# A selective scan on one core: VectorE copies y out of PSUM and makes five of sixteen input products in steps of 256 columns, and softplus is rewritten with tanh

## The chip, the cores and the metric

The kernel runs on one core of one Trainium2 chip. The metric is the device time of one execution in microseconds (us); lower is better. The time before is the median of three runs, 1869.72 us (1868.13 to 1870.24).

## The reference, cut to what matters

The model has two layers, each with cross attention, a mixer and a mixture of experts, over 128 sequences of 32 tokens of width 128. The change lies in the mixer of the second layer, a selective scan ("Mamba" style) with 256 channels, 16 states per channel and a causal convolution of 4 taps. Cut to the lines that the change touches:

```python
dt = jnp.clip(jax.nn.softplus(raw * W_dt + b_dt), 1e-4, 10.0)   # one raw value per token, 256 channels
def step(h, inp):
    dt_t, B_t, C_t, u_t = inp
    dA = jnp.exp(jnp.clip(dt_t[:, :, None] * A, -20.0, 0.0))
    dB_u = jnp.clip(dt_t[:, :, None] * B_t[:, None, :] * u_t[:, :, None], -10.0, 10.0)
    h = jnp.clip(h * dA + dB_u, -100.0, 100.0)
    y = jnp.einsum('bdn,bn->bd', h, C_t)
    return (h, y)
```

The scan runs 32 steps, one after the other. Each step updates 256 x 16 states for each of 128 sequences.

## The kernel before, in words

The kernel goes through its stages one after the other: cross attention, mixer and experts of layer 0, cross attention of layer 1, then the scan stage, then a tail with the experts of layer 1. Between stages all engines meet. An engine works through its own instructions in order, and waits on semaphores that other engines raise. All of that order is written out by hand.

The scan stage (line 1605) has two parts that matter here.

**`scan_inputs`** (line 1620) makes, for each of 32 tiles, the convolved and gated input `u`, the projections `xd` (one raw step size, 16 values of B, 16 of C per token) and the step size `dt`. It is a software pipeline: in one step of the loop, TensorE transposes and convolves one tile, ScalarE applies Silu (L1705) and copies a transpose out of PSUM (L1708), VectorE copies two PSUM results (L1780, L1783), forms the raw `dt` with `scalar_tensor_tensor` (L1785) and normalizes a later tile (`tensor_scalar` of 128 columns with two per-partition operands, L1776), and ScalarE takes the absolute value of the raw `dt` (L1712). GpSimd copies `u` away (L1746) and, in the first 12 tiles, also makes four products for the tail (L1751 to L1756). Behind the loop comes softplus, as max(x, 0) + ln(1 + exp(-|x|)): ScalarE runs Exp and Ln over 2048 columns at a time (L1733, L1737), half of the tiles after the other, and VectorE adds and clips (L1802, L1804).

**`scan_states`** (line 1810) is the scan. A position is one time step. Its 16 states are four groups of four (`q` = 0 to 3), so that a group is 1024 columns. At position `t`:

- ScalarE makes for each group the four decays exp(dt * A) of position `t` (L1897, 256 columns each, into a PSUM ring of three) and, for groups 0 to 2, the four raw products dt*u*B of position `t+1` (L1907). At the end of a position it copies y of position `t-2` out of PSUM (L1913).
- VectorE makes for each group `kept` (L1951, decay times state) and, one group behind, `state` (L1960, add and clip). The raw products of group 3 are VectorE's own: one `tensor_tensor` of 1024 columns, `mine` (L1942), in group 0 of a position.
- GpSimd clips the raw products (`bound`, L1862, 1024 columns), spreads C onto diagonals (`diagonals`, L1867, 512 columns) and makes dt*u of two positions ahead (`dt_u`, L1853), all nine in a fixed order per position: bound 0, diagonal 0, bound 1, diagonal 1, dt_u, bound 2, diagonal 2, bound 3, diagonal 3. A `bound` waits for its raw products.
- TensorE adds up y with the diagonals (L1995). The first group of a position waits until the y buffer of two positions before has been copied out.

`OWN` (L1597) says how many of the four products of each group are VectorE's. `state` of a group waits for `bound`, so for GpSimd; the decays of a group wait for the `state` three groups back, because the PSUM ring has three places.

Of the kernel before, what the change touches and what calls it, by code (L numbers as in the profile page):

```python
# [1619 lines left out]
def scan_inputs(nc, g, uz, dt, xd, a):  # L1620


    with ExitStack() as ctx:
# [25 lines left out]
        waited, abs_sb, exp_sb, ln_sb, soft_sb, clip_sb = (sem(n) for n in ("waited", "abs_sb", "exp_sb", "ln_sb", "soft_sb", "clip_sb"))  # L1649
# [15 lines left out]
        def _(pe):  # L1665
# [30 lines left out]
            pe.wait_ge(prep, TAPS + 2 + 9)  # L1696
# [3 lines left out]
        def _(act):  # L1700
            def step(t, p):
                if inside(t + 1):
                    act.wait_ge(conv_psum, t + 2)
                    wait(act, uz_sb, t)
                    nc.scalar.activation(u[(p + 1) % 2][:, :], c_ps[(p + 1) % 2][:, :], ACT.Silu).then_inc(u_sb, 1)  # L1705
                if inside(t + 2):
                    act.wait_ge(xT_psum, t + 3)
                    nc.scalar.activation(xnT[(p + 2) % TAPS][:, :], x_ps[:, 0:P], ACT.Copy).then_inc(xT_sb, 1)  # L1708
                if inside(t - 2):
                    act.wait_ge(dt_sb, t - 1)  # L1710
                    act.sem_inc(waited, 1)
# [12 lines left out]
            pipeline(act, step, 2, 2, TAPS)  # L1724

            act.wait_ge(abs_sb, T)
            act.wait_ge(a_step, 1)
            nc.scalar.activation(a[:, :], a[:, :], ACT.Exp).then_inc(a_step, 1)
            for half in range(2):
                quarters = range(half * LN_Q // 2, (half + 1) * LN_Q // 2)  # L1730
                for q in quarters:
                    s = slice(q * LT, (q + 1) * LT)
                    nc.scalar.activation(soft[:, s, :], soft[:, s, :], ACT.Exp, scale=-1.0).then_inc(exp_sb, 1)  # L1733
                for q in quarters:
                    s = slice(q * LT, (q + 1) * LT)
# [72 lines left out]


def scan_states(nc, g, uz, dt, xd, a):  # L1810
# [7 lines left out]
    with ExitStack() as ctx:  # L1818
# [69 lines left out]
        def _(act):  # L1888
# [21 lines left out]
            def keep_y(t, k):  # L1910
                act.wait_ge(y_psum, t * NQ + NQ)
                act.sem_inc(waited_act, 1)
                nc.scalar.activation(dt[:, t, :], y_ps[k % 2][:, 0:DI], ACT.Copy).then_inc(y_sb, 1)  # L1913

            def position(t, k, first=False, last=False):
                for q in range(NQ):
# [791 lines left out]
```

## Time and profile before

| | us |
|---|---|
| median of three runs | 1869.72 |
| the profiled execution's own time | 1870.31 |
| span of its profile | 1868.5 |
| TensorE busy in the span | 1580.0 (85%) |
| VectorE busy | 1353.5 (72%) |
| ScalarE busy | 1034.3 (55%) |
| GpSimd busy | 521.2 (28%) |

The profile counts its time from the start of the span. In its views PE is TensorE, DVE VectorE, ACT ScalarE and POOL GpSimd; L1942 is line 1942 of the kernel. Shares over the whole span mix stages with different limits, so the stage of the change has to be read by itself: the input loop lies at about 1030 to 1150 us, softplus at 1150 to 1175 us, the scan at 1175 to 1547 us and the tail behind it.

### The profile page before, as it was taken

Reading aid. Unit: us, or ns where it says so; the run is one execution under the profiler, and the core shown is the slowest. Engines: PE = TensorE matmul, PEld = TensorE weight load, DVE = VectorE, ACT = ScalarE, POOL = GpSimd, SP = SyncE. Lnnn points to the kernel's source line nnn. Section 1 sums busy time; section 2 is a strip of 40 time slices with the busy share of each in tenths; the row PEclk is TensorE's granted clock in tenths of the full one; section 3 lists DMA queues with packets and bytes.
Section 4 is the critical chain, followed back from the end, with each engine's and each line's share of the span. In section 5 each row is a group of like instructions: output and inputs, shape, how many; then the busy total and the mean of one; then the engine's idle time right before and its main releaser. Section 6 shows DMA issues by size and latency. Waiting matters only on the chain. (4 is left out here: it accounts for less than half of the span.)

```text
span 1868.5 us, 36875 instructions
## 1 busy us (share of the span) xinstructions
PE 1580.0 (85%) x10997; PEld 1031.1 (55%) x11024; DVE 1353.5 (72%) x3801; ACT 1034.3 (55%) x2779; POOL 521.2 (28%) x559
## 2 busy tenths in 40 slices
PE   5999999999998999799895885477777774999999
PEld 2666666666665455466563674366655563444444
DVE  4777777777777666577686444799999996677765
ACT  2666666666665333344332225899999992322321
POOL 1211111111111100000000721688888880322200
PEclk9999999999999999899897898798988886999999
DMA  5011011011010900000366000000000001000000
GB/s 136 24 34 34 23 34 34 23 34 34 23 34 5 349 8 0 1 1 1 97 212 183 0 0 0 1 1 0 0 0 0 0 0 51 1 7 6 12 6 17
DMA packets 69336, 66.48 MB, mean 36 GB/s; under 512 B 5695, under 2 KB 66834, under 8 KB 69266
## 3 DMA queue, kind: packets, MB, share of 16 engines
q1 hardware_dynamic: 66598, 64.00, 11.5%
q10 hardware_dynamic: 2668, 1.62, 0.3%
q8 instruction: 35, 0.57, 0.1%
q14 instruction: 35, 0.29, 0.0%
HBM read 61.41 MB, written 4.19 MB: 35 GB/s over the span
## 5 line engine op out<-in xcount | busy, mean ns | idle before, releaser
L1995 PE MATMUL ss_y_ps<-ss_h,ss_diag 128*128 128x256 f32 x1024 | 264.4, 422 | 133.8 <-ACT sc_dt L1913 93.2
L1995 PEld LDWEIGHTS ss_y_ps<-ss_h,ss_diag 128*128 128x128 f32 x1024 | 215.6, 214 | 182.4 <-issue 79.1
L595 ACT ACTIVATE x_probs<-x_probs,x_neg_max 128x257 f32<-128x257 f32 x512 | 253.5, 498 | 63.2 <-DVE x_neg_max L696 63.2
L696 DVE CUSTOM_DVE_ANT_0 x_probs<-x_s_ps,x_mask_b 128x257 f32<-128x257 f32 x512 | 187.3, 423 | 133.5 <-PE x_s_ps L403 133.5
L1897 ACT ACTIVATE ss_decay<-sc_dt,sc_a 128x256 f32 (+1 forms) x496 | 207.8, 479 | 1.8 <-DVE ss_h L1960 1.8
L1951 DVE SCALAR_TENSOR_TENSOR ss_decay<-ss_decay,ss_h 128x1024 f32<-128x1024 f32 x124 | 152.3, 1228 | 27.7 <-ACT ss_decay L1897 27.4
L1907 ACT ACTIVATE ss_come<-ss_dtu,sc_xd 128x256 f32<-128x256 f32 x384 | 163.6, 512 | 6.6 <-POOL ss_dtu L1853 6.6
L413 PE MATMUL x_pT_ps<-all_ident,x_probs 128*128 128x128 f32 x1024 | 162.4, 282 | 0.6 <-DVE x_pT L703 0.6
L1867 POOL TENSOR_TENSOR ss_diag<-all_ident,sc_xd 128x512 f32<-128x512 f32 x128 | 158.8, 1240 | 12.8 <-PE ss_y_ps L1995 2.9
L703 DVE COPY x_pT<-x_pT_ps 128x512 f32<-128x512 f32 x256 | 161.3, 668 | 0.5 <-PE x_pT_ps L413 0.5
L1960 DVE CUSTOM_DVE_ANT_0 ss_h<-ss_come,ss_decay 128x1024 f32<-128x1024 f32 x124 | 149.9, 1209 | 0.0
L319 POOL TENSOR_TENSOR x_rsum_b<-x_rsum,x_one_col 128x512 f32<-128x512 f32 x32 | 33.3, 1041 | 408.7 <-DVE x_rsum L713 408.7
L1862 POOL TENSOR_SCALAR ss_come<-ss_come 128x1024 f32<-128x1024 f32 x124 | 131.3, 1059 | 39.9 <-ACT ss_come L1907 34.3
L413 PEld LDWEIGHTS x_pT_ps<-all_ident,x_probs 128*128 128x128 f32 x1024 | 115.1, 144 | 45.3 <-issue 43.1
L2484 DVE TENSOR_TENSOR tl_scaled<-tl_xnT,tl_w_ps 128x512 f32<-128x512 f32 x96 | 65.4, 687 | 53.0 <-PE tl_w_ps L2200 35.9
L2206 PE MATMUL tl_h_ps<-tl_scaled,tl_w 128*128 128x512 f32 x192 | 98.6, 595 | 0.4
L2206 PE MATMUL tl_y_ps<-tl_scaled,tl_w 128*128 128x512 f32 x192 | 97.5, 592 | 0.8 <-DVE tl_scaled L2484 0.4
L595 ACT ACTIVATION_READ_ACCUMULATOR x_probs<-x_probs,x_neg_max 128x1 f32 x512 | 96.3, 188 | 0.0
L403 PE MATMUL x_s_ps<-x_kT,x_qblk 32*128 32x257 f32 x1024 | 92.7, 431 | 0.0
L390 PE MATMUL x_m_ps<-x_w_qkv,x_ctx_t 128*128 128x128 f32 x512 | 75.1, 291 | 18.2 <-issue 17.2
L430 PE MATMUL x_o_ps<-x_pT,x_v 128*32 128x128 f32 x2048 | 82.5, 279 | 0.9 <-DVE x_pT L703 0.9
L374 PE MATMUL x_m_ps<-x_ctx_t,x_w_qkv 128*128 128x512 f32 x128 | 71.4, 640 | 11.8 <-DVE x_o_norm L719 11.8
(373 smaller groups left out, 3072.0 us busy)
## 6 DMA issues: line engine op xcount, KB each, us to landing
x_ctx_t<-ctxT SPq DMA_DIRECT2D x48, 514.0 KB, 3.8
kept_ctx_t<-ctxT SPq DMA_DIRECT2D x16, 514.0 KB, 8.2
kept_ctx_n<-ctx SPq DMA_DIRECT2D x16, 512.0 KB, 8.5
x_ctx_n<-ctx SPq DMA_DIRECT2D x16, 512.0 KB, 4.1
all_x<-x SPq DMA_DIRECT2D x4, 512.0 KB, 7.8
x_mid<-all_x SPq DMA_DIRECT2D x32, 64.0 KB, 4.0
all_x<-x_mid SPq DMA_DIRECT2D x4, 512.0 KB, 7.6
out<-all_x SPq DMA_DIRECT2D x8, 256.0 KB, 2.0
```

The lines of the kernel that those rows point to most:

```text
L413: ins = tr(pT_ps[u % 2][:, n * P:(n + 1) * P], probs[p][:, 2 * u + j, k * P:(k + 1) * P], g.ident[:, :])
L595: ins = nc.scalar.activation(probs[p][:, n, :], probs[p][:, n, :], ACT.Exp, scale=-1.0, bias=neg_max[p][:, n:n + 1], accum_out=sums[p][:, ...
L696: vec.tensor_tensor_reduce(probs[p][:, n, :], s_ps[:, c, 0:S2], mask_b[:, :], -1.0, -MASKED, ALU.add, ALU.min, neg_max[p][:, n:n + 1]).the ...
L703: vec.tensor_copy(pT[u % 4][:, :], pT_ps[u % 2][:, :]).then_inc(pT_sb, 1)
L1862: nc.gpsimd.tensor_scalar(c[:, :, :], c[:, :, :], 10.0, -10.0, ALU.min, ALU.max).then_inc(bound_sb, 1)
L1867: nc.gpsimd.tensor_tensor(diag[q][:, :, :], g.ident[:, :].unsqueeze(1).to_broadcast([P, NH, P]), c.unsqueeze(2).to_broadcast([P, NH, P]), ...
L1897: ins = nc.scalar.activation(decay[r][:, m * DI:(m + 1) * DI], dt[:, t, :], ACT.Exp, scale=a[:, s:s + 1])
L1907: ins = nc.scalar.activation(come[q][k % 2][:, m, :], dtu[k % 2][:, :], ACT.Copy, scale=xd[:, t, s:s + 1])
L1951: vec.scalar_tensor_tensor(d[:, :], d[:, :], TINY, h[q][:, :, :].rearrange("p m d -> p (m d)"), ALU.max, ALU.mult).then_inc(kept_psum, 1)
L1960: vec._custom_dve(bass.dve_ops.TENSOR_ADD_SAT, out=h[q][:, :, :].rearrange("p m d -> p (m d)"), in0=come[q][k % 2][:, :, :].rearrange("p m ...
L1995: ins = nc.tensor.matmul(y_ps[p][:, 0:DI], diag[q][:, m, :], h[q][:, m, :], start=(q == 0 and m == 0), stop=(q == NQ - 1 and m == NH - 1))
L2206: mm([h_ps, y_ps][j // ME][:, :], w[:, j, :], scaled[j % 4][:, :], start=(j == 0), stop=(j == ME - 1 or j == MC - 1)).then_inc(product, 1)
```

## The change

In the scan, the copy of y moves from ScalarE to VectorE and comes one position earlier (y of `t-1` at the end of position `t`). VectorE's own products become five instead of four: one of group 2 and all four of group 3. Each is now a `tensor_scalar` of 256 columns, with a per-partition operand from `xd` and a `min` with 10, where there was one `tensor_tensor` of 1024 columns. The lone step of group 2 stands in group 0 of a position, the four of group 3 in group 1. ScalarE makes three products of group 2 instead of four.

In the input loop, VectorE clips the raw `dt` (one more `tensor_scalar` of 256 columns) and ScalarE takes Tanh of half the absolute value. With s = 0.5 + 0.5 * tanh(|x|/2), softplus is max(x, 0) - ln(s). So the loop is followed by Ln alone (no Exp), and by one VectorE instruction per quarter instead of two.

```diff
-OWN = (0, 0, 0, 4)
+OWN = (0, 0, 1, 4)
+DT_LOW, DT_HIGH = float(np.log(np.expm1(1e-4))), float(np.log(np.expm1(10.0)))
...
 # scan_inputs, ScalarE, in the loop
                     nc.scalar.activation(soft[:, t - 2, :], dt[:, t - 2, :], ACT.Abs).then_inc(abs_sb, 1)
+                if inside(t - 3):
+                    act.wait_ge(abs_sb, t - 2)
+                    act.sem_inc(waited, 1)
+                    nc.scalar.activation(soft[:, t - 3, :], soft[:, t - 3, :], ACT.Tanh, scale=0.5).then_inc(tanh_sb, 1)
...
 # scan_inputs, ScalarE, behind the loop
-            act.wait_ge(abs_sb, T)
+            for q in range(LN_Q):
+                t = slice(q * LT, (q + 1) * LT)
+                act.wait_ge(tanh_sb, (q + 1) * LT)
+                nc.scalar.activation(soft[:, t, :], soft[:, t, :], ACT.Ln, scale=0.5, bias=half[:, :]).then_inc(ln_sb, 1)
             act.wait_ge(a_step, 1)
             nc.scalar.activation(a[:, :], a[:, :], ACT.Exp).then_inc(a_step, 1)
-            for half in range(2):
...
-                    nc.scalar.activation(soft[:, s, :], soft[:, s, :], ACT.Exp, scale=-1.0).then_inc(exp_sb, 1)
...
-                    nc.scalar.activation(soft[:, s, :], soft[:, s, :], ACT.Ln, bias=1.0).then_inc(ln_sb, 1)
...
 # scan_inputs, VectorE, in the loop and behind it
-                                             ALU.mult, ALU.add).then_inc(dt_sb, 1)
+                                             ALU.mult, ALU.add).then_inc(raw_sb, 1)
+                    dve.wait_ge(raw_sb, t)
+                    vec.tensor_scalar(dt[:, t - 1, :], dt[:, t - 1, :], DT_LOW, DT_HIGH, ALU.max, ALU.min).then_inc(dt_sb, 1)
...
-                vec.scalar_tensor_tensor(dt[:, s, :], dt[:, s, :], 0.0, soft[:, s, :], ALU.max, ALU.add).then_inc(soft_sb, 1)
-                dve.wait_ge(soft_sb, q + 1)
-                vec.tensor_scalar(dt[:, s, :], dt[:, s, :], 1e-4, 10.0, ALU.max, ALU.min).then_inc(clip_sb, 1)
+                vec.scalar_tensor_tensor(dt[:, s, :], dt[:, s, :], 0.0, soft[:, s, :], ALU.max, ALU.subtract).then_inc(soft_sb, 1)
...
 # scan_states, ScalarE
-                    if q == NQ - 1 and not first:
-                        keep_y(t - 2, k)
...
 # scan_states, VectorE
-                m = OWN[q]
-                weight = xd[:, t, 1 + q * NH:1 + q * NH + m]
-                vec.tensor_tensor(come[q][k % 2][:, 0:m, :], dtu[k % 2][:, :].unsqueeze(1).to_broadcast([P, m, DI]),
-                                  weight.unsqueeze(2).to_broadcast([P, m, DI]), ALU.mult).then_inc(mine_sb, 1)
+                for m in range(OWN[q]):
+                    s = 1 + q * NH + m
+                    ins = vec.tensor_scalar(come[q][k % 2][:, m, :], dtu[k % 2][:, :], xd[:, t, s:s + 1], 10.0,
+                                            ALU.mult, ALU.min)
+                ins.then_inc(mine_sb, 1)
+
+            def keep_y(t, k):
+                dve.wait_ge(y_psum, t * NQ + NQ)
+                vec.tensor_copy(dt[:, t, :], y_ps[k % 2][:, 0:DI]).then_inc(y_sb, 1)
...
                     if not last and q < len(BY_DVE):
                         mine(t + 1, k + 1, BY_DVE[q])
+                    if q == NQ - 1:
+                        keep_y(t - 1, k - 1)
```

The rest of the diff is the semaphores' names, a constant tile `half` (one more small memset) and the last y copy.

## Rows read from the trace of the kernel before

**Rows 1.** Busy time by stretch, the scan (stretch, length, engines' busy us, PE clock)
```profile
1175.00:1547.00 372.00, 264.44 (x1024) 215.61 (x1024) 332.02 (x286) 361.74 (x913) 312.12 (x284) 0.89 0.00 0
```
**Rows 2.** Timeline (start us, us, engine, line), ScalarE, one position of the scan
```profile
1381.39 0.40 ACT L1913 ACTIVATE sc_dt<-ss_y_ps 128x256 f32 x1
1381.65 1.69 ACT L1897 ACTIVATE ss_decay<-sc_dt,sc_a 128x256 f32 x4
...
1392.83 0.40 ACT L1913 ACTIVATE sc_dt<-ss_y_ps 128x256 f32 x1
```
**Rows 3.** Timeline, VectorE, in the same position (idle before, releaser in brackets)
```profile
1387.42 1.23 DVE L1951 SCALAR_TENSOR_TENSOR ss_decay<-ss_decay,ss_h 128x1024 f32<-128x1024 f32 x1
1388.56 1.21 DVE L1960 CUSTOM_DVE_ANT_0 ss_h<-ss_come,ss_decay 128x1024 f32<-128x1024 f32 x1
...
1392.96 1.23 DVE L1951 SCALAR_TENSOR_TENSOR ss_decay<-ss_decay,ss_h 128x1024 f32<-128x1024 f32 x1 [0.84 <-ACT ss_decay L1897]
```
**Rows 4.** Timeline, GpSimd, in the same position: bound 1, diagonal 1, dt_u
```profile
1388.49 1.04 POOL L1862 TENSOR_SCALAR ss_come<-ss_come 128x1024 f32<-128x1024 f32 x1
...
1389.62 1.04 POOL L1867 TENSOR_TENSOR ss_diag<-all_ident,sc_xd 128x512 f32<-128x512 f32 x1
...
1390.62 0.74 POOL L1853 TENSOR_TENSOR ss_dtu<-sc_dt,sc_uz 128x256 f32 x1
```
**Rows 5.** Timeline, VectorE's product and GpSimd's diagonal of group 0, in the same position
```profile
1386.28 1.23 DVE L1942 TENSOR_TENSOR ss_come<-ss_dtu,sc_xd 128x1024 f32<-128x1024 f32 x1 [0.15 <-DVE ss_h L1960]
1386.29 2.12 POOL L1867 TENSOR_TENSOR ss_diag<-all_ident,sc_xd 128x512 f32<-128x512 f32 x1
```
**Rows 6.** Timeline, VectorE and GpSimd in the input loop, at three places
```profile
1032.20 0.35 DVE L1776 TENSOR_SCALAR si_xn<-all_x,all_rstd,all_shift 128x128 f32<-128x128 f32 x1 [0.56 <-PE si_x_ps L1672]
...
1053.13 0.61 DVE L1785 SCALAR_TENSOR_TENSOR sc_dt<-si_w_dt,sc_xd,si_b_dt 128x256 f32 x1 [0.16 <-DVE sc_xd L1783]
1053.54 0.79 POOL L1756 TENSOR_TENSOR sc_q<-sc_q,sc_uz 128x256 f32<-128x256 f32 x1
1053.67 0.74 DVE L1776 TENSOR_SCALAR si_xn<-all_x,all_rstd,all_shift 128x128 f32 x1
...
1139.21 0.92 DVE L1785 SCALAR_TENSOR_TENSOR sc_dt<-si_w_dt,sc_xd,si_b_dt 128x256 f32<-128x256 f32 x1
1139.24 0.62 POOL L1746 COPY sc_uz<-si_u 128x512 f32 x1 [2.96 <-ACT si_u L1705]
```
**Rows 7.** Groups of VectorE by line and shape (count | busy us, mean ns | idle before)
```profile
L1780 DVE COPY si_uT<-si_u_ps 128x256 f32<-128x256 f32 x32 | 13.6, 424 | 57.1 <-PE si_u_ps L1687 57.1
...
L1571 DVE TENSOR_SCALAR x_neg<-x_neg,x_c 128x1 f32<-128x1 f32 x32 | 6.9, 214 | 1.1
...
L1804 DVE TENSOR_SCALAR sc_dt<-sc_dt 128x2048 f32<-128x2048 f32 x4 | 4.9, 1227 | 0.1
...
L1981 DVE TENSOR_SCALAR ss_h<-ss_come 128x1024 f32<-128x1024 f32 x4 | 2.7, 692 | 1.9 <-ACT ss_come L1907 1.8
```
**Rows 8.** Timeline from the last step of the input loop to the scan's first instruction
```profile
1149.15 0.42 ACT L1712 ACTIVATE si_soft<-sc_dt 128x256 f32<-128x256 f32 x1 [0.56 <-DVE sc_dt L1785]
...
1156.01 3.71 ACT L1737 ACTIVATE si_soft<-si_soft 128x2048 f32<-128x2048 f32 x2
1157.95 2.29 DVE L1802 SCALAR_TENSOR_TENSOR sc_dt<-sc_dt,si_soft 128x2048 f32<-128x2048 f32 x1 [8.91 <-ACT si_soft L1737]
...
1175.52 1.41 POOL L1853 TENSOR_TENSOR ss_dtu<-sc_dt,sc_uz 128x256 f32<-128x256 f32 x2 [28.69 <-SPq L1818]
```
**Rows 9.** Timeline, the load of a function table in front of the scan's first decays
```profile
1186.07 1.28 ACT L1897 ACT_TABLE_LOAD   x1
```
**Rows 10.** Timeline, Silu in one step of the input loop
```profile
1134.82 0.60 ACT L1705 ACTIVATE si_u<-si_c_ps 128x512 f32<-128x512 f32 x1 [2.51 <-PE si_c_ps L1681]
```
**Rows 11.** Groups of ScalarE: table loads by line (L1259 is a Silu, beside Sigmoid)
```profile
L1259 ACT ACT_TABLE_LOAD x8 | 10.3, 1283 | 0.1
...
L1705 ACT ACT_TABLE_LOAD x1 | 1.3, 1283 | 0.0
```

More of the change, by code:

```diff
@@ L1639, in scan_inputs @@
         soft = sb("soft", [P, T, DI])
+        half = sb("half", [P, 1])
         x_ps, c_ps, u_ps, d_ps = (ps(n, [P, BANK]) for n in ("x_ps", "c_ps", "u_ps", "d_ps"))
@@ L1648, in scan_inputs @@
         waited_pool = sem("waited_pool")
-        waited, abs_sb, exp_sb, ln_sb, soft_sb, clip_sb = (sem(n) for n in ("waited", "abs_sb", "exp_sb", "ln_sb", "soft_sb", "clip_sb"))
+        waited, abs_sb, tanh_sb, ln_sb, soft_sb, raw_sb = (sem(n) for n in ("waited", "abs_sb", "tanh_sb", "ln_sb", "soft_sb", "raw_sb"))
         block = ctx.enter_context(nc.Block())
@@ L1694, in step @@
                     ins.then_inc(xd_psum, 1)
-            pe.wait_ge(prep, TAPS + 2 + 9)
+            pe.wait_ge(prep, TAPS + 3 + 9)
             pipeline(pe, step, 2, 1, TAPS)
@@ L1723, in _ @@
             norm_coefficients(nc, g, act, None, ln_step, lnw)
-            pipeline(act, step, 2, 2, TAPS)
-            act.wait_ge(abs_sb, T)
+            pipeline(act, step, 2, 3, TAPS)
+            for q in range(LN_Q):
+                t = slice(q * LT, (q + 1) * LT)
+                act.wait_ge(tanh_sb, (q + 1) * LT)
+                nc.scalar.activation(soft[:, t, :], soft[:, t, :], ACT.Ln, scale=0.5, bias=half[:, :]).then_inc(ln_sb, 1)
             act.wait_ge(a_step, 1)
             nc.scalar.activation(a[:, :], a[:, :], ACT.Exp).then_inc(a_step, 1)
-            for half in range(2):
-                quarters = range(half * LN_Q // 2, (half + 1) * LN_Q // 2)
-                for q in quarters:
-                    s = slice(q * LT, (q + 1) * LT)
-                    nc.scalar.activation(soft[:, s, :], soft[:, s, :], ACT.Exp, scale=-1.0).then_inc(exp_sb, 1)
-                for q in quarters:
-                    s = slice(q * LT, (q + 1) * LT)
-                    act.wait_ge(exp_sb, q + 1)
-                    nc.scalar.activation(soft[:, s, :], soft[:, s, :], ACT.Ln, bias=1.0).then_inc(ln_sb, 1)
         @block.gpsimd
@@ L1791, in _ @@
             vec.memset(cb[:, :], 0.0).then_inc(prep, 1)
+            vec.memset(half[:, :], 0.5).then_inc(prep, 1)
             dve.wait_ge(w_in, 16 * W_LOADS)
@@ L1795, in _ @@
             vec.tensor_scalar(a[:, :], a[:, :], 5.0, None, ALU.min).then_inc(a_step, 1)
-            dve.wait_ge(prep, 2)
-            split_row(vec, dve, prep, TAPS + 2, cb3[:, :], rowmask, (c_hi[:, :], c_rest[:, :], c_f[:, :]), cb[0:3, :])
+            dve.wait_ge(prep, 3)
+            split_row(vec, dve, prep, TAPS + 3, cb3[:, :], rowmask, (c_hi[:, :], c_rest[:, :], c_f[:, :]), cb[0:3, :])
             pipeline(dve, step, 3, 1, TAPS)
@@ L1801, in _ @@
                 dve.wait_ge(ln_sb, q + 1)
-                vec.scalar_tensor_tensor(dt[:, s, :], dt[:, s, :], 0.0, soft[:, s, :], ALU.max, ALU.add).then_inc(soft_sb, 1)
-                dve.wait_ge(soft_sb, q + 1)
-                vec.tensor_scalar(dt[:, s, :], dt[:, s, :], 1e-4, 10.0, ALU.max, ALU.min).then_inc(clip_sb, 1)
+                vec.scalar_tensor_tensor(dt[:, s, :], dt[:, s, :], 0.0, soft[:, s, :], ALU.max, ALU.subtract).then_inc(soft_sb, 1)
             dve.wait_ge(a_step, 2)
             vec.tensor_scalar(a[:, :], a[:, :], -1.0, None, ALU.mult).then_inc(a_step, 1)
-            dve.wait_ge(clip_sb, LN_Q)
+            dve.wait_ge(soft_sb, LN_Q)
 def scan_states(nc, g, uz, dt, xd, a):
@@ L1908, in raw @@
                 ins.then_inc(raw_sb, 1)
[L1910 to L1913, printed above, removed]
             def position(t, k, first=False, last=False):
@@ L1926, in _ @@
             positions(act, position)
-            keep_y(T - 2, 0)
-            keep_y(T - 1, 1)
         @block.vector
@@ L1985, in _ @@
             state(T - 1, T - 1, L)
+            keep_y(T - 1, T - 1)
+            dve.wait_ge(y_sb, T)
         @block.tensor
```

## The prediction, made before the changed kernel was built

> **What bounds the kernel now.** I read the busy time by stretch first. The scan takes 372 us, and in it ScalarE is busy 361.74, VectorE 332.02 and GpSimd 312.12 us [rows 1]: three engines close together, ScalarE in front. Next I read the timeline of one position. From one y copy on ScalarE to the next are 1392.83 - 1381.39 = 11.44 us [rows 2], which is the period. The y copy itself costs 0.26 (next start minus own start), so the 28 other instructions cost (11.44 - 0.26) / 28 = 0.399 each. ScalarE has no gap; VectorE waits for it, 0.84 us at one place of the position [rows 3]. So ScalarE bounds a position, with VectorE about 1.1 us behind it.
>
> The third view is VectorE and GpSimd beside each other. Some of their instructions exclude one another. The product of 1024 columns (L1942) starts at 1386.28 and takes 1.23; the diagonal that starts 0.01 later takes 2.12 where another takes 1.04 [rows 5, 4]: it has waited for the product's end. The input loop shows the same for a `tensor_scalar` with per-partition operands, the class of instruction that the change puts into the scan: L1776 takes 0.35 alone [rows 6]. Started at 1053.67 beside a GpSimd instruction of 1053.54 to 1054.33, it takes 0.74 and ends at 1054.41, 0.08 after GpSimd's end. `kept` and `state`, which have an operand in PSUM, keep 1.23 and 1.21 beside a busy GpSimd [rows 3, 4].
>
> **The change, part by part.**
>
> *ScalarE in the scan* loses the y copy and one product: 0.26 + 0.40 = 0.66 a position. Its floor becomes 27 x 0.399 = 10.77 us.
>
> *VectorE in the scan, without waits.* An instruction starts 0.09 before the one ahead of it has ended (1387.42 + 1.23 against 1388.56 [rows 3]), so a long one costs 1.14 and eight of them 9.12. The y copy is like L1780, 0.42 [rows 7], so 0.33. A step of 256 columns: the groups of 2048 and 1024 columns give (1227 - 692) / 1024 = 0.52 ns a column and a fixed 157 ns; one column with one operand is 214, so the operand adds 57 [rows 7]. That makes 0.157 + 0.134 + 0.057 = 0.35, or 0.26 in a chain. Five cost 1.30. The sum is 9.12 + 0.33 + 1.30 = 10.75, level with ScalarE's floor. Without any waits, nothing is lost.
>
> The Trainium skill, "VectorE: DVE Perf Modes", in the section on the TRN2 errata, gives 58 + columns/2 cycles for such a copy, and advises tiles of 512 columns and more; at 0.96 GHz that is 0.19 us a step, an estimate. By it the sum would be about 0.3 us a position lower; no row here has a step of just this form.
>
> *VectorE in the scan, with waits.* GpSimd's order is unchanged: eight instructions of 1.04 and one of 0.74 a position, about 0.08 apart [rows 4], some 9.8 us of work. Each of the five steps must find it between two instructions. A step that has waited ends 0.08 + 128 x 0.52 ns = 0.15 after GpSimd's end (the 0.08 from L1776 [rows 6], for 128 columns). The next step starts 0.09 before that, so 0.06 after GpSimd's end; GpSimd's next starts 0.08 after it. Which of the two goes first? L1785, with one operand, started at 1139.21, GpSimd's copy at 1139.24, and L1785 still waited: it took 0.92 and ended 0.27 after the copy [rows 6]. The product without an operand started 0.01 ahead and went first [rows 5]. I read this as the operand's load standing before the claim. So a step with an operand that starts 0.02 ahead loses, and each of the four in the chain waits for one whole GpSimd instruction.
>
> I lay the position out that way. The chain of four falls on diagonal 1, dt_u, bound 2, diagonal 2. The first waits for the rest of a diagonal (0.77, which I take as three quarters), then come one of 0.74 and two of 1.04, each with the gap of 0.08 between GpSimd's instructions: 0.77 + 0.15 + 0.81 + 1.12 + 1.12 = 3.97. The lone step waits for the rest of a diagonal too, 0.81 in all. VectorE: 9.12 + 0.33 + 3.97 + 0.81 = 14.23 a position. It is then the bound, ScalarE waits for `state` through the ring of three, and GpSimd for ScalarE. Against 11.44 that is +2.79 in each of the 30 positions that make a next product: +83.7 us. Bounds, by the first wait of each group (none, or a whole 1.04): 13.0 to 14.8 a position, so +47 to +101.
>
> *The scan's start.* Two of its 24 first products leave ScalarE (0.8), and the table load of 1.28 in front of the first decays [rows 9] goes, because the last function in front of the scan becomes Exp. -2.1; with the load kept, -0.8.
>
> *Softplus.* From the end of the last absolute value (1149.57) to the scan's first instruction (1175.52) are 25.95 us [rows 8]. After: one more VectorE step, a handoff and Tanh at the drain (0.35 + 0.05 + 0.42, about 0.8), a table load 1.28, the first Ln 1.90 (two take 3.71), then four VectorE instructions of 2.29, which are longer than Ln and hide the other three and the Exp of `a`: 9.2; `a` times -1 and the handoff 0.6. Together 13.8, so -12.2. Bounds: if Ln and VectorE did not overlap at all, 5.6 less gain; above, -13.
>
> *The input loop.* ScalarE is idle 2.51 us in each step of 3.58 before Silu [rows 10], so a Tanh of 0.42 fits, taken as 0. VectorE's new clip is one step of 0.35 that can wait for GpSimd's copy (0.62) or product (0.73); the absolute value reads `dt` one step later, so it is covered. While GpSimd is full, in the first 12 tiles, it loses 0.15 a tile at worst: 0 to +2, I take 0.
>
> **Sum.** +83.7 - 2.1 - 12.2 = +69.4 against the profiled execution's 1870.3 us (span 1868.5 and 1.8 around it), so 1939.7. The median of the runs is 0.6 lower: 1939.
>
> **Rivals.**
>
> *The steps of a chain go through together*, VectorE keeping its turn: the race above is 0.02 us. Then a chain costs one wait: 0.92 + 3 x 0.26 = 1.70 and the lone step 0.81, so 11.96 a position, and +15.6 - 2.1 - 12.2 = +1.3: 1871.6, from 1866 to 1882 with the first waits half or full. For it: the product of [rows 5] went first with a lead of 0.01. Against it: L1785 with a lead of 0.03 did not, and L1776 at 1053.67, right behind L1785, let GpSimd in. Chance 0.2, of which 0.09 within 0.2%, 0.07 above and 0.04 below. The Trainium skill, "SBUF — State Buffer" (section "Who interferes with whom"), has a rule for it: whichever issues first gets the shared ports for the whole instruction. By that rule this rival would hold, since the step starts first; the row at 1139.21 speaks against it.
>
> *Faster: the steps find no GpSimd in their way*, because it idles for ScalarE's products when they come (0.2 to 0.65 us at a time, now), or because a `tensor_scalar` of this form doesn't exclude it. Then the floor of 10.77 decides, to about 10.95 with handoffs: 30 x -0.6 = -18, with the rest -32: 1838. It decides once the waits of both groups together stay below 0.9 us a position. Against it: GpSimd works 9.8 us of each position, and the same class waited in [rows 6]. Chance 0.15.
>
> *The change doesn't do what it says in the input loop*: Tanh may not be in Silu's table. Sigmoid and Silu in turn cost a load each time, 8 for L1259 [rows 11]. Two loads of 1.28 and the two functions in the 2.78 us that ScalarE has there would add 0.6 to 2.6 us a step, 19 to 82 us, on top of the forecast: 1958 to 2021. The one load for the loop's Silu, Copy and Abs [rows 11] says nothing of Tanh. Chance 0.05. The Trainium skill, "ScalarE: Activation LUTs" (section "Table sets: the hidden batching unit"), lists tanh beside exp and beside sigmoid and doesn't list Silu's set; no row here shows it.
>
> **How the numbers follow.** The forecast has 0.6: 1939, its own range 1903 to 1957 by the bounds. The range reaches down through the second case, to 1866, and leaves out the faster one and the loads (0.2 together): 1866 to 1957. 0.2% is 3.7 us, about what a measurement here can tell. Faster: 0.15 + 0.04 = 0.19. Same: 0.09. Slower: 0.6 + 0.07 + 0.05 = 0.72.
>
> **What the profile after would show.** Right: 160 `tensor_scalar` of 256 columns on VectorE with a mean near 0.95 us, not 0.35; dt_u on GpSimd 14.2 us apart; ScalarE idle before decays, waiting for `state`; GpSimd idle for ScalarE's products; 13 to 14 us between the loop and the scan; one table load in the loop. Wrong: steps of 0.35, with a period near 10.9 (third case), or one long step in four with a period near 12 (second). Table loads beside Tanh would be the last case.

## The result, and the profile after

The changed kernel takes 1924.1 us (median of four runs, 1921.84 to 1926.92) against 1869.98 for the kernel before (four runs): a ratio of 1.0289, with an interval of 1.027 to 1.0309. It is 54 us slower, where 69 were forecast. The profiled execution has a span of 1920.0 us against 1868.5, so +51.5.

Where these 51.5 us lie is read by cutting the span at the scan's first instruction and at the end of its last y copy. Busy time by stretch of the changed kernel (stretch, length, then busy us with the number of instructions for PE, PE loads, DVE, ACT, POOL, then PE clock): softplus, scan, tail.

```profile
1148.04:1160.80 12.76, 0.00 (x0) 0.00 (x0) 8.98 (x5) 10.46 (x7) 0.00 (x1) 0.50 0.00 0
1160.80:1599.37 438.57, 296.80 (x1024) 231.96 (x1024) 430.19 (x444) 340.94 (x848) 288.22 (x284) 0.84 0.00 0
1599.37:1920.00 320.63, 279.36 (x960) 138.38 (x960) 231.16 (x829) 85.25 (x145) 47.56 (x23) 0.95 0.04 15
```

The scan starts at 1160.80 instead of 1175.52 [rows 8]: 14.7 us earlier. It takes 438.6 us instead of 371.6 (1175.52 to 1547.07 before), so 67.0 more. The tail takes 0.8 less. In the scan of before, ScalarE was busy 361.74 of 372 us [rows 1]; now VectorE is busy 430.19 of 438.57, or 98%, and ScalarE has 98 us of idle time. The bound has moved.

The groups say what fills VectorE and what the others wait for (line, engine, operation, tiles, count | busy us, mean ns | idle before, releaser):

```profile
L1898 ACT ACTIVATE ss_decay<-sc_dt,sc_a 128x256 f32 (+1 forms) x496 | 205.7, 459 | 88.6 <-DVE ss_h L1957 88.6
L1863 POOL TENSOR_SCALAR ss_come<-ss_come 128x1024 f32<-128x1024 f32 x124 | 129.1, 1042 | 130.6 <-ACT ss_come L1908 122.1
L1934 DVE TENSOR_SCALAR ss_come<-ss_dtu,sc_xd 128x256 f32<-128x256 f32 x160 | 140.0, 923 | 1.2 <-POOL ss_dtu L1854 1.2
```

The 160 steps (L1934) have a mean of 0.923 us. ScalarE idles 88.6 us for `state` ahead of decays, GpSimd 122.1 us for ScalarE's products. The timeline shows two positions (start us, us, engine, line; idle before in brackets), VectorE and GpSimd:

```profile
1392.83 0.41 DVE L1940 COPY sc_dt<-ss_y_ps 128x256 f32 x1
...
1394.35 1.04 POOL L1863 TENSOR_SCALAR ss_come<-ss_come 128x1024 f32<-128x1024 f32 x1 [3.60 <-ACT ss_come L1908]
1395.43 0.34 DVE L1934 TENSOR_SCALAR ss_come<-ss_dtu,sc_xd 128x256 f32<-128x256 f32 x1
1395.46 1.21 POOL L1868 TENSOR_TENSOR ss_diag<-all_ident,sc_xd 128x512 f32<-128x512 f32 x1
...
1397.54 1.04 POOL L1863 TENSOR_SCALAR ss_come<-ss_come 128x1024 f32<-128x1024 f32 x1 [0.87 <-ACT ss_come L1908]
1398.02 3.69 DVE L1934 TENSOR_SCALAR ss_come<-ss_dtu,sc_xd 128x256 f32<-128x256 f32 x4
1398.66 1.04 POOL L1868 TENSOR_TENSOR ss_diag<-all_ident,sc_xd 128x512 f32<-128x512 f32 x1
1399.66 0.77 POOL L1854 TENSOR_TENSOR ss_dtu<-sc_dt,sc_uz 128x256 f32 x1
1400.52 1.04 POOL L1863 TENSOR_SCALAR ss_come<-ss_come 128x1024 f32<-128x1024 f32 x1
...
1406.14 0.41 DVE L1940 COPY sc_dt<-ss_y_ps 128x256 f32 x1
...
1408.74 1.23 DVE L1934 TENSOR_SCALAR ss_come<-ss_dtu,sc_xd 128x256 f32<-128x256 f32 x1
1408.77 1.04 POOL L1868 TENSOR_TENSOR ss_diag<-all_ident,sc_xd 128x512 f32<-128x512 f32 x1
...
1411.96 1.04 POOL L1868 TENSOR_TENSOR ss_diag<-all_ident,sc_xd 128x512 f32<-128x512 f32 x1
1412.15 3.99 DVE L1934 TENSOR_SCALAR ss_come<-ss_dtu,sc_xd 128x256 f32<-128x256 f32 x4
...
1414.94 1.04 POOL L1868 TENSOR_TENSOR ss_diag<-all_ident,sc_xd 128x512 f32<-128x512 f32 x1
...
1420.58 0.41 DVE L1940 COPY sc_dt<-ss_y_ps 128x256 f32 x1
```

The chain of four takes 3.69 or 3.99 us. At 1398.02 its steps wait for bound 1 (its rest), diagonal 1, dt_u and bound 2, at 1412.15 for diagonal 1 (its rest), dt_u, bound 2 and diagonal 2, one each. The bounds and diagonals keep their 1.04 there [rows 4]: GpSimd gets its turn after every step. The lone step goes both ways with the same lead of 0.03 us in these rows: at 1395.43 it goes first, takes 0.34, and the diagonal waits (1.21); at 1408.74 it waits for the whole diagonal (1.23). The position takes 13.31 us after a won race and 14.44 after a lost one. From the third y copy to the thirtieth the mean is 13.76; in the kernel before, the same distance is 11.43 to 11.54 as long as a position makes a next product, 11.44 in the mean.

Softplus, from the loop's last Tanh to the scan's first instruction:

```profile
1147.33 0.70 ACT L1718 ACTIVATE si_soft<-si_soft 128x256 f32<-128x256 f32 x2
1148.06 1.28 ACT L1735 ACT_TABLE_LOAD   x1
1149.35 7.68 ACT L1735 ACTIVATE si_soft<-si_soft,si_half 128x2048 f32<-128x2048 f32 x4
1151.38 8.90 DVE L1805 SCALAR_TENSOR_TENSOR sc_dt<-sc_dt,si_soft 128x2048 f32<-128x2048 f32 x4 [4.49 <-ACT si_soft L1735]
...
1157.05 1.28 ACT L1737 ACT_TABLE_LOAD   x1
...
1160.80 1.41 POOL L1854 TENSOR_TENSOR ss_dtu<-sc_dt,sc_uz 128x256 f32<-128x256 f32 x2 [16.76 <-SPq L1819]
```

VectorE's four instructions run 2.03 behind the four Ln and hide the last three of them and the Exp of `a`.

### The profile page after: what moved, and what is told of

It is laid out like the page before. It is cut to its first block and busy times, and to the rows that moved or that the text cites. A ratio compares the mean times of both kernels' runs of the same rounds, so it can differ in the third digit from the quotient of the medians.

```text
span 1920.0 us, 37197 instructions
## 1 busy us (share of the span) xinstructions
PE 1609.8 (84%) x11024; PEld 1044.9 (54%) x11024; DVE 1461.5 (76%) x3990; ACT 1013.2 (53%) x2740; POOL 497.3 (26%) x559
## 5 line engine op out<-in xcount | busy, mean ns | idle before, releaser
L1996 PE MATMUL ss_y_ps<-ss_h,ss_diag 128*128 128x256 f32 x1024 | 296.8, 455 | 156.3 <-DVE ss_h L1957 131.5
L1996 PEld LDWEIGHTS ss_y_ps<-ss_h,ss_diag 128*128 128x128 f32 x1024 | 232.0, 232 | 220.8 <-DVE ss_h L1957 139.3
L1898 ACT ACTIVATE ss_decay<-sc_dt,sc_a 128x256 f32 (+1 forms) x496 | 205.7, 459 | 88.6 <-DVE ss_h L1957 88.6
L1863 POOL TENSOR_SCALAR ss_come<-ss_come 128x1024 f32<-128x1024 f32 x124 | 129.1, 1042 | 130.6 <-ACT ss_come L1908 122.1
L1908 ACT ACTIVATE ss_come<-ss_dtu,sc_xd 128x256 f32<-128x256 f32 x352 | 149.1, 494 | 4.3 <-POOL ss_dtu L1854 4.3
L1934 DVE TENSOR_SCALAR ss_come<-ss_dtu,sc_xd 128x256 f32<-128x256 f32 x160 | 140.0, 923 | 1.2 <-POOL ss_dtu L1854 1.2
L1868 POOL TENSOR_TENSOR ss_diag<-all_ident,sc_xd 128x512 f32<-128x512 f32 x128 | 135.7, 1061 | 12.2 <-PE ss_y_ps L1996 2.3
L2201 PE MATMUL tl_w_ps<-tl_wT,tl_spread 128*128 128x512 bf16 x192 | 74.1, 387 | 14.5 <-DVE tl_scaled L2485 12.4
```

Source lines behind the costliest of these rows:

```text
L1868: nc.gpsimd.tensor_tensor(diag[q][:, :, :], g.ident[:, :].unsqueeze(1).to_broadcast([P, NH, P]), c.unsqueeze(2).to_broadcast([P, NH, P]), ...
L1898: ins = nc.scalar.activation(decay[r][:, m * DI:(m + 1) * DI], dt[:, t, :], ACT.Exp, scale=a[:, s:s + 1])
L1908: ins = nc.scalar.activation(come[q][k % 2][:, m, :], dtu[k % 2][:, :], ACT.Copy, scale=xd[:, t, s:s + 1])
L1934: ins = vec.tensor_scalar(come[q][k % 2][:, m, :], dtu[k % 2][:, :], xd[:, t, s:s + 1], 10.0, ALU.mult, ALU.min)
L1996: ins = nc.tensor.matmul(y_ps[p][:, 0:DI], diag[q][:, m, :], h[q][:, m, :], start=(q == 0 and m == 0), stop=(q == NQ - 1 and m == NH - 1))
```

## The experiments

Twelve kernels were run. The times of before, measured beside each, are 1869.5 (e1 to e4), 1869.6 (e5 to e8), 1866.6 (e9 to e11) and 1867.1 (e12).

| kernel | us | ratio to before | us a position |
|---|---|---|---|
| changed kernel | 1924.1 | 1.0289 [1.027, 1.0309] | 13.31 or 14.44 |
| e1 one product, as before | 1856.1 | 0.9934 [0.9917, 0.995] | 11.46 |
| e2 softplus alone | 1854.8 | 0.9921 [0.9905, 0.9938] | 11.44 |
| e3 steps alone | 1920.8 | 1.0278 [1.0261, 1.0296] | 13.31 |
| e4 y copy alone | 1870.2 | 1.0004 [0.9994, 1.0014] | 11.46 |
| e5 steps with an operand in PSUM | 1853.7 | 0.9916 [0.9899, 0.9932] | 11.34 |
| e6 steps with a constant | 1886.1 | 1.0087 [1.0069, 1.0105] | 12.32 |
| e7 chain alone, in group 0 | 1854.0 | 0.9914 [0.9896, 0.9932] | 11.32 |
| e8 light GpSimd | 1857.6 | 0.994 [0.9924, 0.9957] | 11.44 |
| e9 chain first, then lone step | 1859.0 | 0.9962 [0.9948, 0.9977] | 11.58 |
| e10 all five in group 0 | 1859.9 | 0.9958 [0.9941, 0.9974] | 11.58 |
| e11 chain alone, in group 1 | 1885.2 | 1.0097 [1.008, 1.0114] | 12.46 |
| e12 four steps with PSUM, in group 0 | 1851.4 | 0.9916 [0.9902, 0.9929] | 11.22 |

The last column is the distance of two y copies in most positions; four near the scan's end, behind the loop in the code, take 13.37 in e6 and 12.01 in e8. Where the times of before differ (e9 to e12), kernels are compared by their distance from the time of before that was measured beside each.

**The parts of the change (e1 to e4).** e1 is the changed kernel with

```diff
-OWN = (0, 0, 1, 4)
+OWN = (0, 0, 0, 4)
...
-                for m in range(OWN[q]):
-                    s = 1 + q * NH + m
-                    ins = vec.tensor_scalar(come[q][k % 2][:, m, :], dtu[k % 2][:, :], xd[:, t, s:s + 1], 10.0,
-                                            ALU.mult, ALU.min)
-                ins.then_inc(mine_sb, 1)
+                m = OWN[q]
+                weight = xd[:, t, 1 + q * NH:1 + q * NH + m]
+                vec.tensor_tensor(come[q][k % 2][:, 0:m, :], dtu[k % 2][:, :].unsqueeze(1).to_broadcast([P, m, DI]),
+                                  weight.unsqueeze(2).to_broadcast([P, m, DI]), ALU.mult).then_inc(mine_sb, 1)
```

> The changed kernel with VectorE's products put back to one tensor_tensor of 1024 columns (group 3 alone); the y copy on VectorE and softplus by tanh stay. Theory (each step of 256 columns waits for its own GpSimd instruction): one product waits once at most. ScalarE has 28 instructions a position, 28 x 0.399 = 11.17 us, VectorE 9.12 + 0.33 + 1.14 = 10.6, so ScalarE bounds: 11.2 to 11.5 a position against 11.44 before, with softplus and the table load 14 to 16 us less: 1846 us, from 1844 to 1862. Rival (the y copy on VectorE is what stretches the position, since it waits for TensorE): the period stays above 13, and the time above 1900.

e2 takes `scan_inputs` from the changed kernel and the scan from the kernel before.

> The kernel before with the new input loop and softplus alone. Theory: the stretch from the loop's end to the scan is 13 us instead of 26, the scan's first decays find the table of Exp loaded (1.28 us), the scan's period stays at 11.44: 1854 us, from 1852 to 1858, with the first dt_u near 1160.8. Rival (the clip and Tanh lengthen the input loop): above 1860.

e3 is the kernel before with the changed kernel's `OWN` and the other half of e1's diff, reversed.

> The kernel before with the five steps of 256 columns alone; y copy and softplus as before. Theory: VectorE bounds at the changed kernel's 13.9 us a position less the y copy's 0.33, so 13.5: 30 x 2.1 = 63 us more, 1932 us, from 1920 to 1940. Rival (the y copy is the cost): at most 1885.

e4 is the kernel before with `keep_y` taken from ScalarE's block and put into VectorE's, as in the change.

> The kernel before with the y copy on VectorE alone. Theory: ScalarE loses 0.26 a position and still bounds at 11.2: 30 x 0.26 = 8 us less, 1862 us, from 1860 to 1870. Rival (the y copy waits for TensorE on VectorE and stretches the position): above 1880.

The steps are the cost: alone they add 51.3 us (e3), and without them the changed kernel falls by 68 (e1). Softplus alone gives 14.7 back (e2), as much as the scan's earlier start in the profile. The y copy alone gives nothing (e4), where 8 us were expected. The reason stands in the groups of e4, VectorE's product of 1024 columns and the copy:

```profile
L1933 DVE TENSOR_TENSOR ss_come<-ss_dtu,sc_xd 128x1024 f32<-128x1024 f32 x32 | 57.0, 1783 | 5.7 <-DVE ss_h L1955 4.0 <-POOL ss_dtu L1853 1.2
...
L1938 DVE COPY sc_dt<-ss_y_ps 128x256 f32 x24 | 10.0, 418 | 0.0
```

and in the timeline of e1, whose scan has the same position of 11.46 us:

```profile
1372.13 1.04 POOL L1868 TENSOR_TENSOR ss_diag<-all_ident,sc_xd 128x512 f32<-128x512 f32 x1
1372.44 1.81 DVE L1934 TENSOR_TENSOR ss_come<-ss_dtu,sc_xd 128x1024 f32<-128x1024 f32 x1 [0.16 <-DVE ss_h L1956]
```

In the kernel before the product starts 0.01 ahead of the diagonal and the diagonal pays [rows 5]. With the copy on VectorE the product comes 0.31 behind the diagonal and pays itself: 1.81 instead of 1.23. VectorE then needs 9.12 + 0.33 + 1.72 = 11.17, and two short idle times (0.16 and 0.02 us, each with the overlap of 0.09 lost) bring it to about 11.5; ScalarE's 0.26 is lost again. So, by the trace, the copy was not free.

The three parts don't add up: -14.7 + 51.3 + 0.7 = +37, and together they measure +54. In e3 the thirty lone steps take 0.36 to 0.45, but for a first of 0.92, and the positions 13.2 to 13.3; in the changed kernel 14 of 30 lose and take 1.15 to 1.23. A lone step of e3 with GpSimd beside it (timeline; its line is L1942, bound and diagonal are L1862 and L1867):

```profile
1387.13 1.04 POOL L1862 TENSOR_SCALAR ss_come<-ss_come 128x1024 f32<-128x1024 f32 x1 [2.73 <-ACT ss_come L1907]
1387.89 0.43 DVE L1942 TENSOR_SCALAR ss_come<-ss_dtu,sc_xd 128x256 f32<-128x256 f32 x1
1388.26 1.04 POOL L1867 TENSOR_TENSOR ss_diag<-all_ident,sc_xd 128x512 f32<-128x512 f32 x1
```

It starts 0.28 before bound 0 ends, waits for that rest only, and is through when the diagonal comes. In the changed kernel the step starts 0.04 after bound 0 has ended (1395.43 against 1394.35 + 1.04), later by about the 0.33 of the copy, and so meets the diagonal. Fourteen lost races of 14.44 - 13.31 = 1.13 would be 16 us; the scans of the two profiles are 12.9 us apart (438.6 against 425.7).

**Is it GpSimd's turn, or the step itself (e5, e8)?** e5 is the changed kernel with

```diff
-                    ins = vec.tensor_scalar(come[q][k % 2][:, m, :], dtu[k % 2][:, :], xd[:, t, s:s + 1], 10.0,
-                                            ALU.mult, ALU.min)
+                    ins = vec.scalar_tensor_tensor(come[q][k % 2][:, m, :], dtu[k % 2][:, :], xd[:, t, s:s + 1],
+                                                   ten[:, 0:DI], ALU.mult, ALU.min)
```

where `ten` is a PSUM bank full of 10.0. Both y buffers become one bank (TensorE waits for the copy of `t-1` instead of `t-2`), and the y copy stands behind group 2.

> The changed kernel with the same five steps as scalar_tensor_tensor whose third operand, the constant 10, lies in PSUM (both y buffers become one bank to make room, and the y copy stands one group earlier). Theory (steps with all operands in SBUF exclude GpSimd's instructions, those with one in PSUM do not): a step takes 0.4 to 0.5 us by its own columns (half the rate: 0.157 + 0.267 + 0.057 = 0.48) and never waits, VectorE 9.12 + 0.33 + 2.0 = 11.45 a position, diagonals on GpSimd 1.04: 1870 - 15 + 1 = 1856 us, from 1850 to 1875. Rival (steps of 256 columns with a per-partition operand cost 0.9 in this place by themselves): mean still 0.9, time 1910 or more.

e8 cuts GpSimd's work:

```diff
-                nc.gpsimd.tensor_scalar(c[:, :, :], c[:, :, :], 10.0, -10.0, ALU.min, ALU.max).then_inc(bound_sb, 1)
+                nc.gpsimd.tensor_scalar(c[:, 0:1, :], c[:, 0:1, :], 10.0, -10.0, ALU.min, ALU.max).then_inc(bound_sb, 1)
...
+                n = NH if isinstance(t, int) else 1
-                nc.gpsimd.tensor_tensor(diag[q][:, :, :], g.ident[:, :].unsqueeze(1).to_broadcast([P, NH, P]),
+                nc.gpsimd.tensor_tensor(diag[q][:, 0:n, :], g.ident[:, :].unsqueeze(1).to_broadcast([P, n, P]),
```

> The changed kernel with GpSimd's work cut to a quarter: its clip takes one of a group's four products and its diagonals one of four, in the same order and number of instructions (leaves out the clip of the other products and fresh C for the other diagonals). Theory: a step waits for a GpSimd instruction of some 0.3 us instead of 1.04, or finds none: mean 0.4 to 0.6 us, and the position falls to ScalarE's floor and the handoffs, 10.9 to 11.8: 1838 to 1866 us. Rival (steps are slow by themselves): mean 0.9, time above 1910.

The steps' group in e5, and a chain of e5 beside GpSimd:

```profile
L1934 DVE SCALAR_TENSOR_TENSOR ss_come<-ss_dtu,sc_xd,ss_ten 128x256 f32<-128x256 f32 x160 | 67.2, 464 | 0.5 <-POOL ss_dtu L1854 0.5
```
```profile
1385.63 1.04 POOL L1863 TENSOR_SCALAR ss_come<-ss_come 128x1024 f32<-128x1024 f32 x1 [1.04 <-ACT ss_come L1908]
1386.18 1.64 DVE L1934 SCALAR_TENSOR_TENSOR ss_come<-ss_dtu,sc_xd,ss_ten 128x256 f32<-128x256 f32 x4
1386.75 1.04 POOL L1868 TENSOR_TENSOR ss_diag<-all_ident,sc_xd 128x512 f32<-128x512 f32 x1
```

The same product over as many columns, in the same place of a position, takes 0.464 beside a busy GpSimd, against 0.923; and GpSimd keeps 1.04. The Trainium skill, "SBUF — State Buffer" (section "Who interferes with whom"), says that a VectorE instruction with at most one input in SBUF and outside the two-port modes doesn't contend with GpSimd; these rows agree, if the per-partition operand doesn't count as such an input. These steps are another instruction than those of the changed kernel, so e5 alone doesn't exclude the form as the cause. In e8, with the form unchanged, the steps' mean falls to 0.50 and the time to 66 us under the changed kernel's, with as many GpSimd instructions in the same order. So the rival of slow steps falls.

**Is it the operand's load that loses the turn (e6)?** One line of the changed kernel:

```diff
-                    ins = vec.tensor_scalar(come[q][k % 2][:, m, :], dtu[k % 2][:, :], xd[:, t, s:s + 1], 10.0,
+                    ins = vec.tensor_scalar(come[q][k % 2][:, m, :], dtu[k % 2][:, :], 0.5, 10.0,
```

> The changed kernel with a constant 0.5 in place of the per-partition operand of the five steps (leaves B out of these products). Theory (the load of that operand lets GpSimd claim first, so that a step loses the turn to GpSimd each time): the steps of a chain go through together behind one wait, 1.7 us a chain, so 12.0 a position or the 11.2 to 11.5 that the floors allow: 1862 us, from 1850 to 1875. Rival (GpSimd gets its turn between any two VectorE instructions, operand or not): mean of a step stays at 0.85 to 0.95 us, time 1915 to 1926.

The time falls by 38 us and lies between the two expectations. The second step of a chain, in the changed kernel first, then the second and third step in e6 (timeline):

```profile
1398.65 1.20 DVE L1934 TENSOR_SCALAR ss_come<-ss_dtu,sc_xd 128x256 f32<-128x256 f32 x1
```
```profile
1377.69 0.28 DVE L1934 TENSOR_SCALAR ss_come<-ss_dtu 128x256 f32<-128x256 f32 x1
1377.70 1.16 POOL L1868 TENSOR_TENSOR ss_diag<-all_ident,sc_xd 128x512 f32<-128x512 f32 x1
...
1377.89 1.13 DVE L1934 TENSOR_SCALAR ss_come<-ss_dtu 128x256 f32<-128x256 f32 x1
```

Both second steps start 0.01 ahead of the diagonal (1398.66 and 1377.70). With the operand the step loses the turn and takes 1.20; without it, it wins, takes 0.28, and the diagonal waits. It is no single pair: taken to the nanosecond, all 59 steps of the changed kernel that start at most 0.015 us ahead of a GpSimd instruction lose, and all 30 steps of e6 that start 0.010 to 0.018 ahead win. So the operand decides this race, as the prediction had read from L1785 [rows 6]. It doesn't decide the next: the diagonal, now waiting, goes in behind the second step, and the third waits 1.13. A chain takes 2.69, not 1.7: one turn of four is won. The Trainium skill's rule in the section named above, that whoever issues first gets the ports, holds for the step with a constant and, at a lead this short, not for the step with an operand, by these two rows.

**The lone step, or the place of the chain (e7, e9 to e11)?** e7 is the changed kernel with

```diff
-OWN = (0, 0, 1, 4)
+OWN = (0, 0, 0, 4)
```

> The changed kernel without the lone step of group 2 (ScalarE makes all four products of group 2; the four steps of group 3 stay, and move to group 0 of a position). Theory: the chain of four costs 3.7 to 4.0 as now, the lone step's mean of some 0.75 goes: 13.1 a position, 30 x 0.75 = 22 us under the changed kernel, 1902 us, from 1894 to 1910. Rival (the lone step's wait only moves to the chain, which then waits longer): within 6 us of the changed kernel.

It gives 70 us instead of 22: both expectations were wrong. By the code, dropping the lone step moves the chain, too: `mine` of the first group in `BY_DVE` stands in group 0 of a position, that of the second in group 1. A chain of e7:

```profile
1385.54 1.04 POOL L1868 TENSOR_TENSOR ss_diag<-all_ident,sc_xd 128x512 f32<-128x512 f32 x1
...
1385.99 1.52 DVE L1934 TENSOR_SCALAR ss_come<-ss_dtu,sc_xd 128x256 f32<-128x256 f32 x4 [0.17 <-DVE ss_h L1957]
...
1387.60 1.04 POOL L1863 TENSOR_SCALAR ss_come<-ss_come 128x1024 f32<-128x1024 f32 x1 [1.03 <-ACT ss_come L1908]
```

The first step waits for the rest of the diagonal. Behind it GpSimd has nothing ready: its next `bound` waits 1.03 us for ScalarE's products, and three steps pass in that gap at 0.34 each. e11 takes e7 and moves the chain back:

```diff
-                    if not last and q < len(BY_DVE):
-                        mine(t + 1, k + 1, BY_DVE[q])
+                    if not last and q == 1:
+                        mine(t + 1, k + 1, BY_DVE[0])
```

> The kernel of e7 (four steps, no lone step), with the chain moved back to group 1 of a position. Theory (place): in group 1 GpSimd has diagonal, dt_u and bound ready one behind the other and takes its turn after every step, 3.7 to 4.0 us a chain; in group 0 of e7 it waits for ScalarE's products and the chain takes 1.52. VectorE 9.12 + 0.33 + 3.7 to 3.9 = 13.2 a position: 1905 us, from 1890 to 1912. Rival (the lone step, by its delay in group 0, is what makes the chain long): as e7, 1850 to 1858.

A chain of e11:

```profile
1394.08 2.84 DVE L1934 TENSOR_SCALAR ss_come<-ss_dtu,sc_xd 128x256 f32<-128x256 f32 x4
1394.73 1.04 POOL L1868 TENSOR_TENSOR ss_diag<-all_ident,sc_xd 128x512 f32<-128x512 f32 x1
...
1395.73 0.78 POOL L1854 TENSOR_TENSOR ss_dtu<-sc_dt,sc_uz 128x256 f32 x1
...
1396.80 1.04 POOL L1863 TENSOR_SCALAR ss_come<-ss_come 128x1024 f32<-128x1024 f32 x1 [0.29 <-ACT ss_come L1908]
```

The place alone costs 34 us (18.6 above the kernel before, where e7 is 15.5 below it). The size was overrated: three turns are lost, not four, because bound 2 still waits 0.29 for ScalarE and the fourth step finds the gap. In the changed kernel that gap is gone, too: VectorE is slower by the lone step, ScalarE is ahead, bound 2 follows dt_u without a wait (1400.52), and the fourth step loses as well. In these two kernels the VectorE that is further behind has closed the gap in which its step would pass.

e9 and e10 keep all five steps. e9 reverses their order, so that the chain stands in group 0 and the lone step in group 1:

```diff
-BY_DVE = [q for q in range(NQ) if OWN[q] > 0]
+BY_DVE = [q for q in range(NQ) if OWN[q] > 0][::-1]
```

> The changed kernel with its five steps in the other order: the chain of four in group 0, the lone step of group 2 in group 1. Theory (place): the chain takes 1.5 to 2.5 us, the lone step waits for a whole GpSimd instruction, 0.7 to 1.2; VectorE 9.12 + 0.33 + 1.5 to 2.5 + 0.6 to 1.1 = 11.5 to 13.0 a position: 1872 us, from 1856 to 1900. Rival (five steps cost five turns wherever they stand): 1915 or more.

e10 is e9 with both calls of `mine` in group 0:

```diff
-                    if not last and q < len(BY_DVE):
-                        mine(t + 1, k + 1, BY_DVE[q])
+                    if not last and q == 0:
+                        for d in BY_DVE:
+                            mine(t + 1, k + 1, d)
```

> The changed kernel with all five steps in group 0. Theory (place): 1.52 as in e7 and one step of 0.26 more, 1.8, if GpSimd's next bound comes after the fifth: VectorE 11.2 a position, 1850 us; one turn lost to that bound (ScalarE has 0.4 us a position less to do now, so its products come earlier) adds 0.9 a position: 1876. Range 1846 to 1885. Rival (five turns wherever they stand): 1915 or more.

The timeline of e9:

```profile
1387.45 1.77 DVE L1934 TENSOR_SCALAR ss_come<-ss_dtu,sc_xd 128x256 f32<-128x256 f32 x4 [0.17 <-DVE ss_h L1957]
...
1389.32 1.04 POOL L1863 TENSOR_SCALAR ss_come<-ss_come 128x1024 f32<-128x1024 f32 x1 [1.03 <-ACT ss_come L1908]
...
1391.41 0.34 DVE L1934 TENSOR_SCALAR ss_come<-ss_dtu,sc_xd 128x256 f32<-128x256 f32 x1
1391.44 0.90 POOL L1854 TENSOR_TENSOR ss_dtu<-sc_dt,sc_uz 128x256 f32 x1
```

The chain passes in the gap of 1.03 us, and the lone step wins its race: dt_u waits (0.90 instead of 0.74). The same instructions in another order take 62 us less than the changed kernel (7.6 below the kernel before, against 54.1 above it). Their number is not the cost; their order is. e10 says the same: its first step waits for the rest of a diagonal and the other four pass in that gap, 2.04 us a position in all.

**A version faster than the changed kernel and the kernel before (e12).** e5 with `OWN = (0, 0, 0, 4)`, so that the chain stands in group 0 and has an operand in PSUM.

> The kernel of e5 (steps with the constant in PSUM) without the lone step: ScalarE makes all of group 2, VectorE the four of group 3, in group 0 of a position. Theory: the steps exclude nothing, 1.64 us a chain; VectorE 9.12 + 0.33 + 1.55 = 11.0, ScalarE 28 x 0.399 = 11.17 and some 0.1 of waits, so 11.25 a position against 11.34 in e5 and 11.33 in e7: 3 us less than those, 1851 us, from 1848 to 1855, the fastest of all. Rival (a third wait decides both, for TensorE's y or between VectorE and ScalarE): 1853 to 1857, as e5 and e7.

```profile
1200.00:1500.00 300.00, 220.41 (x864) 181.49 (x862) 295.51 (x349) 299.99 (x750) 240.77 (x242) 0.89 0.00 0
```

In this stretch of its scan ScalarE is busy 299.99 of 300 us again. A position takes 11.22 us, near ScalarE's 28 x 0.399 = 11.17, and 0.1 less than in e5 and e7. The ratio can't be told from theirs, so the 3 us that were expected are not shown by the times. Of what e5, e7 and e12 have below the kernel before, 15.5 to 15.9 us, the 14.7 of e2 are softplus.

## Why the prediction was right, point by point

**The bound.** It held: VectorE 98% busy, ScalarE idle ahead of decays, GpSimd idle ahead of `bound`.

**The chain of four.** Forecast 3.97 us, on diagonal 1, dt_u, bound 2 and diagonal 2. Measured 3.99 on just these after a lost lone step, 3.69 after a won one, where the chain comes earlier and its first wait is the rest of bound 1; 3.76 in the mean. That 3.99 came so near is in part luck: the rest of the diagonal was 0.85 (1411.96 + 1.04 - 1412.15), not the 0.77 that was taken, and the gap of 0.08 isn't there between diagonal 1 and dt_u. dt_u starts 0.04 before the diagonal has ended (1389.62 + 1.04 against 1390.62 [rows 4]), which the prediction misread. The turns are lost one by one, and where step and GpSimd stand 0.01 us apart, it is by the operand (e6).

**The lone step.** Forecast 0.81. Measured in the mean 0.74, but as two values: 0.34 in 16 positions of 30, 1.15 to 1.23 in the other 14. No lone step took 0.81, so the near mean is luck.

**A step by itself.** Forecast 0.35. It takes 0.34 where GpSimd is out of its way (e7), so the 0.19 that stands beside it in the prediction doesn't hold here. That 0.19 was a whole duration, set against 0.26 with the overlap of 0.09 taken off; like with like, it would have made the sum 0.8 us a position lower, not 0.3.

**The position.** The mis-sized term. The forecast added up 9.12 + 0.33 + 3.97 + 0.81 = 14.23 with the steps' whole durations, though it had found that an instruction starts 0.09 before the one ahead of it ends. With that taken off both groups and the measured durations, 9.12 + 0.33 + (3.76 - 0.09) + (0.74 - 0.09) = 13.77, and the trace has 13.76. The 0.46 between them are 0.21 for the chain, 0.07 for the lone step and 0.18 for the overlap; over 30 positions they are 14 of the 14.6 us by which the scan's 67.0 fall short of the forecast 81.6 (83.7 - 2.1).

**ScalarE's 0.66 a position.** True of its work (340.94 us busy against 361.74, 0.69 in each of 30 positions), and worth nothing in the changed kernel, where VectorE bounds. Of the y copy alone the expectation of e4 said 8 us, and e4 shows none.

**Softplus.** Forecast -12.2; the scan starts 14.7 earlier, and e2 is 14.7 faster. From the end of the last absolute value (about 1147.4) to 1160.80 are 13.4 us against the 13.8 forecast, so the stretch was priced well; the other 2 us are a loop that ends earlier. They are within what the stages ahead vary: the first dt_u comes at 1172.45 to 1175.52 in the three kernels with the old input stage (before, e3, e4).

**The scan's start.** Forecast -2.1, with 1.28 for the table load. The load is gone in e2, and its scan is 0.2 us shorter, no more (371.36 against 371.56): the load was worth nothing there. No run has the other 0.8 by itself.

**The rivals.** The chain goes through together: not here, but it does where GpSimd has nothing ready (e7, e9). The faster case named that condition, GpSimd idle for ScalarE's products; e9 shows that it is met in group 0. Its 1838 did not come even so. VectorE's floor of 10.75 equals ScalarE's 10.77, so every wait counts: in e9 the first step's wait of 0.65 and the handoff of 0.17 make 11.57 of 10.75, its position takes 11.58, and it takes 1859. The point of 0.9 us from which that case was to decide was set too high for a gain over 11.44; it is 11.44 - 10.75 = 0.69. Table loads beside Tanh: none; the loop's one load serves Silu, Copy, Abs and Tanh.

**What the prediction didn't see** is that the place of the chain makes the loss. It looked for what GpSimd runs in group 1, rightly, and took that as given for any place.

## What to carry to other kernels

Short VectorE instructions with all operands in SBUF and one of them per partition cost up to a GpSimd instruction each beside a GpSimd that always has one ready, so price them by GpSimd's queue at their place, not by their columns: in this kernel one long instruction waited once, four short ones up to four times. Put such a chain where GpSimd waits for another engine (here 62 us for a reversed list), or give it an operand in PSUM (0.464 us a step in e5). After moving any instruction between engines, read again who starts first in every such pair: a copy of 0.42 us changed a race and gave back all that it saved (e4).

## What the runs showed of the hardware that was not expected

- The lone step's race turns on hundredths of a microsecond. With the starts taken to the nanosecond, 25 of the 30 lone steps of the changed kernel start ahead of a GpSimd instruction: the 12 with a lead of 0.037 us or more all won, of the 13 with 0.031 to 0.036 four won and nine lost. The other five start 0.035 to 0.042 behind the diagonal and lost. Both steps shown lead by 0.036, so what decides there stays open. Against dt_u less was enough: in e9 all 27 lone steps with a lead of 0.023 to 0.034 won.
- A per-partition operand cost a step twice: 0.34 instead of 0.28 us by itself (e6), and the turn against a bound or a diagonal where the lead was 0.01 us (1.20 instead of 0.28).
- The slower form was the faster one: a step with an operand in PSUM takes 0.464 in the mean of e5, one with all operands in SBUF 0.34 with GpSimd out of its way, but 0.923 in the mean of the changed kernel.
